# Softmax attention on one core: where the small products stand between the maxima

## The chip, the cores and the metric

The kernel runs on one core of a Trainium2 chip. The metric is the device time of one execution in microseconds (us); lower is better. Engines: PE is TensorE, DVE is VectorE, ACT is ScalarE, POOL is GpSimd, SP is SyncE.

## The reference

A decoder block of two layers over 1024 tokens (2 sequences of 512) of width 512, in float32. Six parts follow each other, each as `x = x + part(layernorm(x))`: a gated mixer, cross attention (softmax), a mixture of experts, decayed linear attention, linear cross attention, and a block-scaled feed forward. The change is in the second part:

```
q = qdq(x) @ qdq(wq).T + bq;  k, v = split(ctx @ wkv.T + bkv)      # 16 heads of 32, 1024 keys for each sequence
attn = softmax(q k^T / sqrt(32));  o = attn @ v
out = qdq(o) @ qdq(wp).T + bp        # qdq: each row to int8 by its largest magnitude, and back
x = x + out                          # then the layernorm of the experts
```

## The kernel before

**Groups, pairs, super-steps.** `cross_attention` (from L679) works on 8 groups `g`: sequence `g // 4`, four heads each. A group is two pairs of heads, so there are 16 pairs. A pair has 8 tiles of 128 keys for each of two heads. A *super-step* is 4 tiles of scores; a group has 8 super-steps, the whole attention 64 (numbered 0 to 63 here). A *slot* is half a super-step: super-step s has slots 2s and 2s+1, a group 16 slots.

**What PE does in a super-step** (the loop `for ss in range(NSS + 1)`, just after L1098): two score products (L1084), the jobs of slot 2s, two score products, the jobs of slot 2s+1, and then the eight products of probabilities and values (`weigh`, L1098) of the super-step before. ACT takes the exponential of each score tile (L1220) from a ring of three PSUM banks.

**The jobs.** The scores need the row maxima of the logits one group ahead. For that there are 16 units `max` for each group: PE makes 128x1024 logits (two products, L844), DVE reduces them to 128 maxima (L856, `b_nm`). In slots 10 to 105 nearly every slot has one. Other jobs use the same banks: `turn` (PE transposes the maxima of a group, L851; DVE splits them, L864 and L866, and ends with a small memset, L869), `pair` (four transposes of a finished pair's result, L1068; DVE divides by the sums, L1474 and L1477), `spread`, `oturn` (four transposes of the rounded output of a token tile, L1030; DVE copies them, L1465), `oproj` (the output projection of a token tile, four bf16 products, L1035; DVE scales it, L1406), `xturn` (four transposes of a normalised token tile, L1042; DVE copies them, L1469). `oturn`, `oproj` and `xturn` are those of tiles 0 to 3, the first sequence, which is finished halfway; the other four tiles come after the attention.

**The two job banks.** Jobs are numbered in the order of the list `JOBS`. Job j uses bank pair `2 * (j % 2)`, and PE may not start it before DVE has read job j-2:

```
if j >= 2:
    pe.wait_ge(job_read, j - 1)
```

PE and DVE both run through `JOBS` in order. After the jobs of a slot DVE does that slot's *step*, if `STEPS_AT` has one: the maxima of an output row, its scales, `rounded` (two operations, L1400 and L1403), `residual` (adds the projection to x, L1411), `stats` (L1415, L1417), `variance`, `normed` (L1425), `bias` (L1448), `most`. `oturn` waits on PE for `rounded` of its tile, `xturn` for `normed`. POOL takes the power for the normalisation in its turn for group 6, between two copies of values; SP sends the rows of maxima to the scores' operands after each `turn` (L836) and stacks the next group's operands (L826, L829).

**Placement before.** A slot's jobs are appended in the order `max`, `pair`, `turn`, `spread`, `oturn`, `oproj`, `xturn`. Slots counted from 64 (group 4): `oturn` of tiles 0 to 3 in 11, 12, 13, 14; `oproj` in 15, 17, 19, 21; `xturn` in 37, 38, 39, 40. The `turn` of the next group stands in the 13th slot of a group (12 counted from 0), behind that slot's `max`; the first of them in slot 13.

Of the kernel before, what the change touches and what calls it, by code (L numbers as in the profile page):

```python
# [678 lines left out]
def cross_attention(c):  # L679
# [70 lines left out]
    NG, QT = len(GROUPS), BANK // P  # L750
# [15 lines left out]

    SLOTS = 2 * TURNS_PER * 2
    LEAD, TURN_AT = 6, 12
    JOBS, JOBS_AT = [("max", 0, u) for u in range(UNITS)] + [("turn", 0, 0)], []
    FIRST_JOBS = len(JOBS)  # L770

    def first_slot(g, u):
        return SLOTS * (g - 1) - LEAD + u if g > 1 else 1 + 12 * u // UNITS

    for slot in range(2 * NSS + 5):
        g, here = slot // SLOTS, len(JOBS)
        JOBS += [("max", gg, u) for gg in range(1, NG) for u in range(UNITS) if first_slot(gg, u) == slot]
        q = (slot - 3) // (2 * TURNS_PER) - 1
        if slot == 2 * (TURNS_PER * (q + 1) + 1) + 1 and 0 <= q < PAIRS:
            JOBS.append(("pair", q, 0))  # L780
        if g + 1 < NG and slot % SLOTS == (TURN_AT if g else 13):
            JOBS.append(("turn", g + 1, 0))
        if slot == 20:
            JOBS.append(("spread", 0, 0))
        if g == 4 and 11 <= slot % SLOTS < 15:
            JOBS.append(("oturn", slot % SLOTS - 11, 0))
        if slot in range(4 * SLOTS + 15, 4 * SLOTS + 23, 2):
            JOBS.append(("oproj", (slot - 4 * SLOTS - 15) // 2, 0))
        if g == 6 and 5 <= slot % SLOTS < 9:
            JOBS.append(("xturn", slot % SLOTS - 5, 0))  # L790
        JOBS_AT.append(range(here, len(JOBS)))
    LAST_PAIR = len(JOBS) - 1


    STEPS_AT = {4 * SLOTS + at: step for at, step in
                [(4 + t, ("maxima", t)) for t in range(4)] + [(8, ("scales", 0))] + [(9 + t, ("rounded", t)) for t in range(4)]
                + [(16 + 2 * t, ("residual", t)) for t in range(4)] + [(23 + t, ("stats", t)) for t in range(4)]
                + [(27, ("variance", 0))] + [(34 + t, ("normed", t)) for t in range(4)]
                + [(60 + t, ("most", 4 + t)) for t in range(4)]
                + [(24 + 2 * t - 4 * SLOTS, ("bias", t)) for t in range(TT)]}  # L800

# [5 lines left out]
    added, stats_done, aggr_done, var_done, rstd_done, normed = (  # L807
        c.sem(f"c_ln_{n}") for n in ("added", "stats_done", "aggr_done", "var_done", "rstd_done", "normed"))
# [2494 lines left out]


STAGES = [mixer, cross_attention, linear_attention, mx_feed_forward]


# [77 lines left out]
```

## Time and profile before

| | us |
|---|---|
| median of 3 runs | 1894.0 |
| lowest and highest | 1892.58, 1895.92 |
| the profiled execution, its own time | 1895.18 |
| span from the first to the last instruction in it | 1893.4 |

| engine | busy us | share of the span |
|---|---|---|
| PE | 1833.2 | 97% |
| DVE | 1229.8 | 65% |
| ACT | 713.2 | 38% |
| POOL | 376.7 | 20% |

Times in rows are counted from the span's start. Busy time on PE is modelled: matmuls are pipelined, and a row's duration holds the tail of its last matmul, under which the next instruction can start already. So the distance between two starts says what an instruction really takes, and an idle time is shorter than the delay it stands for. "x8" is eight instructions merged into a row; a few per cent of matmul records can be missing, so that a row says x3 where four were run. Attention's super-steps lie between 304.8 and 595.4 us.

### The profile page before, as it was taken

What the parts mean: (1) busy time and instruction counts of PE and PEld (TensorE: products, weight loads), DVE (VectorE), ACT (ScalarE), POOL (GpSimd) and SP (SyncE); (2) the same over time, 40 slices, a digit from 0 to 9 for tenths busy, and PEclk for the clock granted to TensorE, in tenths of its full rate; (3) what the DMA queues carried; (4) which work ended last, traced back from release to release, by engine and by line L of the source; (5) the groups of instructions that cost most, each with busy time, mean ns of one, the idle gap of its engine ahead of it and who ended that gap; (6) DMA issues with size and microseconds to landing.
All of it is one profiled execution on the core that took longest, in us unless ns stands there. A gap on an engine that the chain in (4) does not pass through costs nothing. (4 is left out here: it accounts for less than half of the span.)

```text
span 1893.4 us, 24735 instructions
## 1 busy us (share of the span) xinstructions
PE 1833.2 (97%) x9384; PEld 1381.7 (73%) x9388; DVE 1229.8 (65%) x2114; ACT 713.2 (38%) x1151; POOL 376.7 (20%) x286
## 2 busy tenths in 40 slices
PE   8999999999899999999999999999999999999998
PEld 6888786444344688678887888887888865888886
DVE  6435665666743666686787786787782367666656
ACT  4302333455354588533333333332344332322211
POOL 0000011121100488511211211211110001144532
PEclk9999999999999899999999999999999999999999
DMA  6102323233314111232314313314112110110101
GB/s 223 45 1 72 100 63 80 53 76 76 96 26 134 34 68 57 89 120 53 100 40 121 102 40 124 100 40 137 49 65 78 69 45 22 45 45 23 45 1 45
DMA packets 109049, 132.67 MB, mean 70 GB/s; under 512 B 36066, under 2 KB 72930, under 8 KB 107394
## 3 DMA queue, kind: packets, MB, share of 16 engines
q1 hardware_dynamic: 108932, 131.10, 22.6%
q8 instruction: 75, 1.23, 0.3%
q14 instruction: 42, 0.34, 0.1%
HBM read 97.27 MB, written 14.75 MB: 59 GB/s over the span
## 5 line engine op out<-in xcount | busy, mean ns | idle before, releaser
L856 DVE TENSOR_REDUCE b_nm<-ps 128x1 f32<-128x1024 f32 x128 | 153.5, 1220 | 82.2 <-PE ps L844 82.2
L1220 ACT ACTIVATE b_pr<-ps 128x512 f32<-128x512 f32 x256 | 133.4, 602 | 127.7 <-PE ps L1084 127.4
L253 PE MATMUL ps<-d_x_high,d_w_high 128*128 128x512 f32 x384 | 154.3, 402 | 1.7 <-issue 1.7
L255 PE MATMUL ps<-d_x_high,d_w_low 128*128 128x512 f32 x384 | 149.8, 390 | 0.0
L254 PE MATMUL ps<-d_x_low,d_w_high 128*128 128x512 f32 x384 | 149.7, 390 | 0.0
L2487 POOL TENSOR_TENSOR d_sqsum<-d_sqsum,d_sq 128x512 f32<-128x512 f32 x32 | 45.1, 1409 | 474.4 <-ACT d_sq L2398 474.2
L1098 PE MATMUL ps<-b_pr,b_VS 128*64 128x512 f32 x512 | 123.8, 605 | 0.0
L1810 POOL TENSOR_TENSOR c_h<-c_h,c_w_row 128x512 f32<-128x512 f32 x64 | 105.5, 1658 | 29.6 <-DVE c_h L1825 20.3
L1084 PEld LDWEIGHTS ps<-b_qS,b_kS 98*128 98x128 f32 x256 | 42.6, 188 | 69.5 <-issue 49.5
L1084 PE MATMUL ps<-b_qS,b_kS 98*128 98x512 f32 x256 | 90.5, 435 | 2.8 <-ACT b_pr L1220 2.6
L844 PE MATMUL ps<-b_kS,b_qS 96*128 96x512 f32 x256 | 81.6, 402 | 7.8 <-DVE b_nm L856 6.2
L253 PEld LDWEIGHTS ps<-d_x_high,d_w_high 128*128 128x128 f32 x384 | 72.2, 188 | 17.4 <-issue 2.1
L255 PEld LDWEIGHTS ps<-d_x_high,d_w_low 128*128 128x128 f32 x384 | 72.1, 188 | 15.5
L254 PEld LDWEIGHTS ps<-d_x_low,d_w_high 128*128 128x128 f32 x384 | 72.3, 188 | 13.5
L1098 PEld LDWEIGHTS ps<-b_pr,b_VS 128*64 128x64 f32 x512 | 31.1, 136 | 55.5 <-issue 51.2
L1825 DVE TENSOR_TENSOR c_h<-ps,c_sq 128x512 f32<-128x512 f32 x64 | 44.3, 692 | 41.6 <-PE ps L255 24.7
L2380 ACT ACTIVATE d_kF<-ps 128x512 f32<-128x512 f32 x32 | 19.1, 598 | 131.9 <-PE ps L255 131.9
L844 PEld LDWEIGHTS ps<-b_kS,b_qS 96*128 96x128 f32 x256 | 46.4, 190 | 22.1 <-DVE b_nm L856 13.6
L3240 ACT ACTIVATE f_hF_high<-ps 128x512 fp32r<-128x512 f32 x32 | 19.1, 599 | 115.2 <-PE ps L3084 115.2
L2608 DVE TENSOR_TENSOR d_y<-ps,d_y 128x512 f32<-128x512 f32 x48 | 33.2, 692 | 43.9 <-PE ps L255 43.9
L3062 DVE TENSOR_TENSOR f_h<-ps,f_silu 128x512 f32<-128x512 f32 x32 | 21.8, 680 | 55.5 <-PE ps L255 32.2
L2281 PE MATMUL ps<-d_A,d_v 128*64 128x128 f32 x512 | 49.6, 284 | 4.4 <-DVE d_S L2562 4.4
(466 smaller groups left out, 4968.5 us busy)
## 6 DMA issues: line engine op xcount, KB each, us to landing
b_kS<-b_k_parts SPq DMA_DIRECT2D x96, 128.0 KB, 2.3
f_rows<-d_fw SPq DMA_DIRECT2D x24, 512.0 KB, 2.8
f_w<-f_rows SPq DMA_DIRECT2D x12, 1024.0 KB, 4.8
c_w_row<-w_rows SPq DMA_DIRECT2D x16, 512.0 KB, 3.6
b_qS<-b_q_parts SPq DMA_DIRECT2D x96, 64.0 KB, 2.0
d_w<-in_d_wq SPq DMA_DIRECT2D x16, 256.0 KB, 2.9
d_w<-in_d_wk SPq DMA_DIRECT2D x16, 256.0 KB, 3.0
d_w<-in_d_wg SPq DMA_DIRECT2D x16, 256.0 KB, 3.7
```

The source lines that it names most:

```text
L253: nc.tensor.matmul(out, lhsT[0], rhs[0], start=start, stop=False)
L254: nc.tensor.matmul(out, lhsT[0], rhs[1], start=False, stop=False)
L255: return nc.tensor.matmul(out, lhsT[1], rhs[0], start=False, stop=stop)
L844: last = nc.tensor.matmul(c.ps[:, banks + n, :], qS[s_][0:96, h, t * P:(t + 1) * P], kS[s_][0:96, h, n * BANK:(n + 1) * BANK], start=True, ...
L856: nc.vector.tensor_reduce(nm[:, g % 2, u:u + 1], c.ps[:, banks:banks + 2, :], AX.XY, ALU.max, negate=True).then_inc(job_read, 1)
L1084: nc.tensor.matmul(c.ps[:, 4 + n % BANKS, :], kS[g % 2][0:98, h, k * P:(k + 1) * P], qS[g % 2][0:98, h, :], start=True, stop=True).then_in ...
L1098: last = nc.tensor.matmul(c.ps[2 * DH * hh:2 * DH * (hh + 1), 7, :], VS[:, 2 * (q % 2) + hh, k * VW:k * VW + VPAD], pr[:, (n + hh) % RING, :],
L1220: nc.scalar.activation(pr[:, n % RING, :], c.ps[:, 4 + n % BANKS, :], ACT.Exp).then_inc(exp_done, 1)
L1810: nc.gpsimd.tensor_tensor(h[j % HR][:], h[j % HR][:], head.w_row[e % 2][:, n * BANK:(n + 1) * BANK], ALU.mult).then_inc(hw_done, 1)
L1825: nc.vector.tensor_tensor(h[j % HR][:], c.ps[:, 2 + j % 2, :], sq[:, j % 2, :], ALU.mult).then_inc(h_done, 1)
L2281: last = nc.tensor.matmul(c.ps[hh * D:(hh + 1) * D, 6 + b, col], v[:, t, h * D:(h + 1) * D], A[:, b, hh, ch, :], start=ch == 0, stop=True, ...
L2487: nc.gpsimd.tensor_tensor(sqsum[:, tok], sqsum[:, tok], sq[:, b, :], ALU.add).then_inc(sqsum_done, 1)
```

## The change

Three things. First, `turn`, `oturn`, `oproj` and `xturn` are appended ahead of the slot's `max`, not behind it. Second, they get even slots, so that at most one of them stands in a super-step, between its first two score products and its first `max`. Counted from slot 64: `oturn` 10, 14, 16, 18; `oproj` 20, 22, 24, 26; `xturn` 46, 48, 50, 52 (where no `max` is left). The turns of the maxima keep their slots. Third, DVE's steps behind them move: `residual` to 21, 23, 25, 29; `stats` to 31, 33, 37, 39; `variance` to 40; `normed` to 42 to 45. `pair` jobs stay where they were, behind the second `max`. The instructions of the kernel are the same in number and form.

```diff
     LEAD, TURN_AT = 6, 12
+    OTURN_AT, OPROJ_AT, XTURN_AT = (10, 14, 16, 18), (20, 22, 24, 26), (46, 48, 50, 52)
...
     for slot in range(2 * NSS + 5):
         g, here = slot // SLOTS, len(JOBS)
+        if g + 1 < NG and slot % SLOTS == (TURN_AT if g else 13):
+            JOBS.append(("turn", g + 1, 0))
+        if slot - 4 * SLOTS in OTURN_AT:
+            JOBS.append(("oturn", OTURN_AT.index(slot - 4 * SLOTS), 0))
+        if slot - 4 * SLOTS in OPROJ_AT:
+            JOBS.append(("oproj", OPROJ_AT.index(slot - 4 * SLOTS), 0))
+        if slot - 4 * SLOTS in XTURN_AT:
+            JOBS.append(("xturn", XTURN_AT.index(slot - 4 * SLOTS), 0))
         JOBS += [("max", gg, u) for gg in range(1, NG) for u in range(UNITS) if first_slot(gg, u) == slot]
         q = (slot - 3) // (2 * TURNS_PER) - 1
         if slot == 2 * (TURNS_PER * (q + 1) + 1) + 1 and 0 <= q < PAIRS:
             JOBS.append(("pair", q, 0))
-        if g + 1 < NG and slot % SLOTS == (TURN_AT if g else 13):
-            JOBS.append(("turn", g + 1, 0))
         if slot == 20:
             JOBS.append(("spread", 0, 0))
-        if g == 4 and 11 <= slot % SLOTS < 15:
-            JOBS.append(("oturn", slot % SLOTS - 11, 0))
-        if slot in range(4 * SLOTS + 15, 4 * SLOTS + 23, 2):
-            JOBS.append(("oproj", (slot - 4 * SLOTS - 15) // 2, 0))
-        if g == 6 and 5 <= slot % SLOTS < 9:
-            JOBS.append(("xturn", slot % SLOTS - 5, 0))
...
-                + [(16 + 2 * t, ("residual", t)) for t in range(4)] + [(23 + t, ("stats", t)) for t in range(4)]
-                + [(27, ("variance", 0))] + [(34 + t, ("normed", t)) for t in range(4)]
+                + [(at, ("residual", t)) for t, at in enumerate((21, 23, 25, 29))]
+                + [(at, ("stats", t)) for t, at in enumerate((31, 33, 37, 39))]
+                + [(40, ("variance", 0))] + [(42 + t, ("normed", t)) for t in range(4)]
```

## Rows read from the trace of the kernel before

**Rows 1.** Windows: stretch, its length, busy us of each engine, granted clock, DMA.

```profile
470.95:553.92 82.97, 74.41 (x323) 34.76 (x323) 58.63 (x83) 35.48 (x68) 9.76 (x13) 1.00 0.29 74
595.40:700.00 104.60, 104.02 (x420) 70.75 (x420) 69.23 (x126) 64.86 (x102) 52.56 (x30) 0.95 0.30 93
```

**Rows 2.** Waits of PE in 470.95 to 553.92: total, times, longest.

```profile
PE ps L1030 <- DVE b_nm L856: 2.5, 2, 1.3
```

**Rows 3.** Timeline of PE: an undisturbed super-step (34 to 35), start and duration.

```profile
463.05 0.73 PE L1084 MATMUL ps<-b_qS,b_kS 98*128 98x512 f32 x2
463.63 0.63 PE L844 MATMUL ps<-b_kS,b_qS 96*128 96x512 f32 x2
465.13 1.94 PE L1098 MATMUL ps<-b_pr,b_VS 128*64 128x512 f32 x8
467.00 0.73 PE L1084 MATMUL ps<-b_qS,b_kS 98*128 98x512 f32 x2
```

**Rows 4.** Timeline of PE: super-step 37, its oturn, and the start of 38.

```profile
475.46 0.40 PE L1030 MATMUL ps<-identb,b_oq 128*128 128x128 bf16 x4 [1.33 <-DVE b_nm L856]
...
477.65 0.73 PE L1084 MATMUL ps<-b_qS,b_kS 98*128 98x512 f32 x2
```

**Rows 5.** Timeline of DVE: the operations of jobs and steps.

```profile
471.29 0.50 DVE L1403 TENSOR_SCALAR b_oq<-b_o 128x512 bf16<-128x512 f32 x1
...
474.18 1.22 DVE L856 TENSOR_REDUCE b_nm<-ps 128x1 f32<-128x1024 f32 x1
...
493.63 0.74 DVE L1406 SCALAR_TENSOR_TENSOR b_tmp<-ps,b_so,b_swp_row 128x512 f32<-128x512 f32 x1
...
559.44 0.06 DVE L869 MEMSET b_mark<- 1x1 f32 x1
```

**Rows 6.** Timeline of PE: an oproj and the weigh behind it.

```profile
492.04 1.04 PE L1035 MATMUL ps<-b_wpT,b_oqF 128*128 128x512 bf16 x4 [0.38 <-DVE b_nm L856]
493.01 1.94 PE L1098 MATMUL ps<-b_pr,b_VS 128*64 128x512 f32 x8
```

**Rows 7.** Timeline of PE: starts of super-steps 45 and 46; 45 has a pair.

```profile
515.45 0.73 PE L1084 MATMUL ps<-b_qS,b_kS 98*128 98x512 f32 x2
...
520.42 0.73 PE L1084 MATMUL ps<-b_qS,b_kS 98*128 98x512 f32 x2
```

**Rows 8.** Timeline of PE: super-step 14 with its turn; later group 7's.

```profile
371.32 0.73 PE L1084 MATMUL ps<-b_qS,b_kS 98*128 98x512 f32 x2
...
373.83 0.73 PE L844 MATMUL ps<-b_kS,b_qS 96*128 96x512 f32 x2 [0.74 <-DVE b_nm L856]
...
376.36 0.74 PE L1084 MATMUL ps<-b_qS,b_kS 98*128 98x512 f32 x2
...
558.48 0.27 PE L851 MATMUL ps<-ident,b_nm 128*16 128x128 f32 x1
```

**Rows 9.** Timeline of PE: super-step 6 with the turn of group 1.

```profile
337.31 0.74 PE L844 MATMUL ps<-b_kS,b_qS 96*128 96x512 f32 x2 [0.39 <-DVE b_nm L856]
338.44 0.28 PE L851 MATMUL ps<-ident,b_nm 128*16 128x128 f32 x1 [0.40 <-DVE b_nm L856]
338.65 1.94 PE L1098 MATMUL ps<-b_pr,b_VS 128*64 128x512 f32 x8
```

**Rows 10.** Timeline of PE: an xturn and the scores behind it (super-step 51).

```profile
544.34 0.60 PE L1042 MATMUL ps<-ident,xn 128*128 128x128 f32 x4
544.70 0.71 PE L1084 MATMUL ps<-b_qS,b_kS 98*128 98x512 f32 x2
```

**Rows 11.** Timeline of PE: super-step 55, after the last max, and the next.

```profile
561.39 0.96 PE L1084 MATMUL ps<-b_qS,b_kS 98*128 98x512 f32 x3
562.58 0.49 PE L1084 MATMUL ps<-b_qS,b_kS 98*128 98x512 f32 x1 [0.22 <-ACT b_pr L1220]
...
564.87 0.96 PE L1084 MATMUL ps<-b_qS,b_kS 98*128 98x512 f32 x3
```

**Rows 12.** Windows after the attention, with the granted clock.

```profile
625.00:630.00 5.00, 5.00 (x21) 4.58 (x22) 2.53 (x3) 3.96 (x4) 2.07 (x1) 0.50 0.00 0
```

## The prediction

> **What bounds the kernel now.** I read the page first: PE is busy 97% of the span, so only what PE does or waits for can move the end. The windows come next: super-steps 37 to 52 are the stretch from 470.95 to 553.92, 82.97 us with 74.41 of PE busy, while DVE has 58.63 [rows 1]. In such a stretch the reader should look at the waits: two `oturn` alone wait 2.5 us there for DVE's maxima [rows 2]. Last, the timeline gives the yardstick. An undisturbed super-step takes 467.00 - 463.05 = 3.95 us, and its first maximum starts 463.63 - 463.05 = 0.58 after it [rows 3]. Sixteen of these would be 63.2 us, so the stretch holds 82.97 - 63.2 = 19.8 us of extras: four `pair`, two `turn`, four `oturn`, four `oproj`, four `xturn`, and the waits among them.
>
> **Why it waits.** A job needs DVE to have read the job before the last. DVE wants about 1.2 us for a maximum [rows 5]; two maxima fill 2.4 of the 3.95 us, so single ones never hold PE up. But a small job behind a maximum follows it on PE after half a microsecond and then needs the reading of the other bank, and DVE's step lies before that reading too. In super-step 37 three jobs and a step come together: `oturn` starts only at 475.46 after 1.33 us idle, and the super-step lasts 477.65 - 470.95 = 6.70 us, 2.75 over [rows 1, 4]. Put before the first maximum, a job has the `weigh` products (465.13 to 467.00, 1.87 us) and two scores (0.58) between it and the last job, 2.4 us in which DVE catches up [rows 3].
>
> **Own cost of each job on PE**, from starts:
> - `oproj`: 493.01 - 492.04 = 0.97 us [rows 6].
> - `xturn` between maximum and scores: 544.70 - 544.34 = 0.36 us [rows 10]; before `weigh` I take 0.5, between that and its row's 0.60.
> - `oturn`: bf16, row 0.40 us long [rows 4]. It lies between 0.2 (the 0.60 row of `xturn` costs 0.36, so 0.24 of a row is tail) and 0.4; I take 0.25.
> - `turn`: one matmul, 0.27 us long [rows 8], nearly all tail: 0.03.
> - `pair`: super-step 45 lasts 520.42 - 515.45 = 4.97, so 1.02 each with its wait; it stays in place and keeps it [rows 7].
>
> **The stretch before, split.** 4 pairs 4.1, 4 oproj 3.9, 4 oturn 1.0, 4 xturn (two at 0.36, two at 0.5) 1.7, turns 0.1: 10.8 us. Of 19.8 that leaves 9.0 us of waits.
>
> **The stretch after, by super-steps.**
> - 37 (`oturn` 0; two maxima; pair): the products are ready at 470.95 + 0.58 = 471.53, but `oturn` needs `rounded` of tile 0, which ends 471.29 + 0.50 = 471.79 [rows 5], so 0.3 of wait. DVE then has a copy (about 0.4), a maximum, `rounded` (about 0.95), a maximum, the pair's two operations. The pair waits only for the first maximum, at about 473.95, and `weigh` follows 0.6 later; 5.5 us in all.
> - 38 (`turn` 5, no `oturn`): DVE is still behind with `rounded`, and reaches the turn's reading about 0.1 late: 4.3 us.
> - 39 (`oturn` 1): DVE reads the last maximum of 38 to 0.9 after the start of 39; the first maximum waits 0.15: 4.4 us.
> - 40 and 41 (`oturn` 2, 3): 3.95 + 0.25 = 4.2, and with the pair 5.2.
> - 42 to 44 (`oproj` 0 to 2): 3.95 + 0.97 = 4.9 each. DVE's scaling (0.74 [rows 5]) starts when the product ends and is over as the second maximum comes up, so no wait. DVE has two maxima 2.4, scaling 0.7, `residual` 0.6 in it, 3.7 of 4.9.
> - 45 (`oproj` 3, pair): 4.97 + 0.97, and 0.2 because the scaling delays the maximum for which the pair waits: 6.1.
> - 46 (`turn` 6): 4.1. 49 has its pair, 4.97. The six others (47, 48, 50, 51, 52 and no `xturn` any more) are five at 3.95: 19.75.
>
> Sum: 5.5 + 4.3 + 4.4 + 4.2 + 5.2 + 14.7 + 6.1 + 4.1 + 4.97 + 19.75 = 73.2 us. Gain 82.97 - 73.2 = **9.8 us**: 8.0 of waits, the rest the `xturn`s gone elsewhere.
>
> **The xturns' new place** (super-steps 55 to 58). There a super-step lasts 564.87 - 561.39 = 3.48 us and PE waits 0.22 for ACT before the fourth score [rows 11]. An `xturn` of 0.36 between the score pairs uses that wait up: 0.14 is left. Bounds 0 and 0.5; four times 0.1 to 0.14 is **+0.4 us** (up to 2.0). Its `normed` comes four slots earlier on a DVE without maxima, so it never waits. POOL's power is released later by `variance` (slot 104, not 91), and behind it in POOL's queue stand only the values of pair 14, whose buffer is not free before super-step 53; cost nothing. No DMA moves but the rows of maxima behind `turn`, which go out earlier. SP's loads of the next operands hang on scores that come sooner too; the nearest deadline is group 7's first stacking, released in super-step 43 and needed in 45, and there `oproj` gives it 9.8 us where it had 7.9. Bound: 0 to 1.2 us, I take 0.
>
> **The turns of groups 2, 3, 4** (turns 5 and 6 are counted). Super-step 14 lasts 376.36 - 371.32 = 5.04 us, 1.09 over, because the second maximum stands at 373.83 and waits for the turn's reading, which DVE can do only after the first maximum [rows 8]. In front, DVE reads the turn at once (group 7's turn, with no maximum about, starts at 558.48 and its reading is over at 559.44 + 0.06, 1.02 us later [rows 5, 8]), and the second maximum comes 0.03 + 0.47 + 0.57 = 1.07 after it. So 4.0 us, gain 1.05 each: **-3.1 us** for three. If DVE is 0.3 later it is 2.2.
>
> **The turn of group 1** stands in an odd slot. Now the maximum starts at 337.31 and the turn at 338.44 [rows 9]. Swapped, the maximum gets the later start, and 0.5 to 0.65 lie between it and `weigh` instead of 338.65 - 338.44 = 0.21: **+0.4 us**.
>
> **Sum**: -9.8 + 0.4 - 3.1 + 0.4 = -12.1 us, taken as -12. Behind the attention PE is busy 104.02 of 104.60 us [rows 1], so the rest shifts as a whole. The profiled execution, 1895.2 us of its own time (1.8 over its span), would come to 1883.2; it stood 1.2 over the median of 1894.0, so the forecast for the median is **1882 us**. Own range 1879 to 1885: turns 0.9 less, `oturn` and DVE's lag 1.5 either way, xturns up to 1.6 more, loads up to 1.2.
>
> **Where the clock could come in.** All of 470.95 to 553.92 has clock 1.00 [rows 1]; after the attention the row at 625 to 630 shows 0.50, the 1.2 GHz level, behind transposes between products of 16 columns [rows 12]. Such a fall of some 8 us comes again and may take 4 us more or less with where it falls.
>
> The Trainium skill ("TensorE: Matmul & The Clock Gate", Part 4: PE-mode transpose) says that transposes do not count as busy for the clock in the way that products do; by that rule the change spreads transposes into the stretch paced by ACT, where PE has the least work. No row of that stretch shows it; it is the last rival below.
>
> **Rivals.**
> 1. *DVE becomes the bound between slots 74 and 93.* For: rounding, copies and two maxima make 0.4 + 2.4 + 0.95 (twice at worst) on DVE in a super-step of 4.2, so each maximum may carry a lag over. Against: 58.63 of 82.97 us busy [rows 1]. Eight super-steps losing 0.7 more each: 5.6 less gained, 1887.6 us.
> 2. *The gain is given back* by something with a time of its own behind the attention, as weights that arrive late. Against: PE's 104.02 of 104.60. Time: 1894. That the order doesn't change what PE waits for would show the same.
> 3. *The clock falls in super-steps 55 to 63*, the other side. At 0.50 the `weigh` (1.87) and the four scores (0.96) double: 2.8 us for each super-step. It decides from the fifth such super-step on (12 / 2.8 = 4.3); with all ten from 554 on the price is 28: 1910 us. For: `pair`s there already put transposes beside a wait of 0.22, and now four more come. Against: four times 0.36 us is little in 40 us.
>
> **How the numbers follow.** Forecast 0.68, rival 1 0.19, rival 2 0.06, rival 3 0.05, something slower otherwise 0.02. What a measurement can tell is 0.2%, 3.8 us. Faster: the forecast, rival 1 but a sliver: 0.86; same 0.07; slower 0.07. The range takes in half of rival 1 above and the clock's luck below: 1877.5 to 1888.5.
>
> **What would show it.** PE's waits on `b_nm` at L1030, L1035 and at L844 behind `turn` go from 9 us to near 1; super-step 14 goes to 4.0; those with `oproj` to 4.9; 37 to 5.5; xturns cost under 0.2. It is wrong if the super-steps with a job in front last over 0.5 longer than I say (rival 1), if the attention is 12 us shorter and the end is not (rival 2), or if the clock shows 0.50 before 595 (rival 3).

## The result, and the profile after

The median went from 1894.1 to **1880.5 us**; the ratio is 0.9926 with a 95% interval of 0.9907 to 0.9945, that is 10 to 18 us faster. One of the four executions after the change took 9052.4 us at a granted clock of 0.189, for a reason that no profile shows, and is left out of the ratio; the other three took 1877.3, 1880.3 and 1880.8. The forecast was 1882. The profiled execution took 1877.3 us (span 1875.5).

Lines after the change stand two lower than before (L844 is L846, L856 L858, L1030 L1032, L1035 L1037, L1042 L1044, L1068 L1070, L1084 L1086, L1098 L1100). First the windows of super-steps 37 to 52, to be set against [rows 1]. Columns: stretch, length, busy us of PE, of the weight loads (PEld), of DVE, ACT and POOL, granted clock, DMA share, GB/s:

```profile
468.24:541.67 73.43, 71.58 (x307) 33.12 (x307) 54.39 (x76) 35.97 (x68) 9.39 (x13) 1.00 0.33 83
```

The stretch lasts 73.43 us where it lasted 82.97, with four xturns fewer in it. PE is busy for all but 1.85 us of it; before, 8.56 us were idle. PE's waits in that stretch, all there are, against [rows 2]:

```profile
PE ps L1070 <- DVE b_nm L858: 1.5, 4, 0.4
PE ps L1032 <- DVE b_oq L1405: 0.3, 1, 0.3
```

No `oturn` and no `oproj` waits for maxima any more. What is left are the pairs (L1070), which the change did not touch, and one `oturn` for its rounding. The timeline of PE shows super-step 37, then 38, against [rows 4]:

```profile
468.24 0.73 PE L1086 MATMUL ps<-b_qS,b_kS 98*128 98x512 f32 x2
469.23 0.38 PE L1032 MATMUL ps<-identb,b_oq 128*128 128x128 bf16 x4 [0.26 <-DVE b_oq L1405]
469.42 0.71 PE L846 MATMUL ps<-b_kS,b_qS 96*128 96x512 f32 x2
469.97 0.63 PE L1086 MATMUL ps<-b_qS,b_kS 98*128 98x512 f32 x2
470.44 0.63 PE L846 MATMUL ps<-b_kS,b_qS 96*128 96x512 f32 x2
471.45 0.66 PE L1070 MATMUL ps<-ident,b_oT 128*128 128x128 f32 x4 [0.38 <-DVE b_nm L858]
472.04 1.94 PE L1100 MATMUL ps<-b_pr,b_VS 128*64 128x512 f32 x8
473.90 0.73 PE L1086 MATMUL ps<-b_qS,b_kS 98*128 98x512 f32 x2
```

The idle of 1.33 before `oturn` is now 0.26, and the super-step went from 6.70 to 5.66 us. In super-step 14, with rows of PE, PEld and DVE, the turn stands first and DVE reads it ahead of the maximum (against [rows 8]):

```profile
371.57 0.73 PE L1086 MATMUL ps<-b_qS,b_kS 98*128 98x512 f32 x2
...
372.14 0.27 PE L853 MATMUL ps<-ident,b_nm 128*16 128x128 f32 x1
...
372.17 0.71 PE L846 MATMUL ps<-b_kS,b_qS 96*128 96x512 f32 x2
...
372.76 0.28 DVE L868 TENSOR_TENSOR b_nm_parts<-ps,b_nm_parts 16x128 fp32r<-16x128 f32 x1
...
373.08 1.22 DVE L858 TENSOR_REDUCE b_nm<-ps 128x1 f32<-128x1024 f32 x1
373.09 0.06 DVE L871 MEMSET b_mark<- 1x1 f32 x1
373.20 0.30 PEld L846 LDWEIGHTS ps<-b_kS,b_qS 96*128 96x128 f32 x2 [0.27 <-DVE b_mark L871]
373.21 0.73 PE L846 MATMUL ps<-b_kS,b_qS 96*128 96x512 f32 x2
...
373.87 1.94 PE L1100 MATMUL ps<-b_pr,b_VS 128*64 128x512 f32 x8
...
375.74 0.73 PE L1086 MATMUL ps<-b_qS,b_kS 98*128 98x512 f32 x2
```

The reading ends at 373.15, and the second maximum starts 0.06 later. PE shows no idle there, but the load of its weights waits 0.27 us for the reading: the maximum still comes a little late, and the super-step lasts 4.17 us, not 4.0. And an xturn in super-step 55 (against [rows 11]):

```profile
549.14 0.73 PE L1086 MATMUL ps<-b_qS,b_kS 98*128 98x512 f32 x2
549.71 0.60 PE L1044 MATMUL ps<-ident,xn 128*128 128x128 f32 x4
550.07 0.76 PE L1086 MATMUL ps<-b_qS,b_kS 98*128 98x512 f32 x2
550.75 1.94 PE L1100 MATMUL ps<-b_pr,b_VS 128*64 128x512 f32 x8
552.62 0.73 PE L1086 MATMUL ps<-b_qS,b_kS 98*128 98x512 f32 x2
```

552.62 - 549.14 = 3.48 us, as long as without the xturn; the wait for ACT is gone.

**The yardstick for the experiments.** Outside low-clock stretches the length of a super-step repeats from trace to trace to 0.03 us in all but a few places, so the traces say far more than the times. I take the *attention length*: from the first score product to the first product of the experts' logits. Before, the rows are

```profile
304.78 0.86 PE L1084 MATMUL ps<-b_qS,b_kS 98*128 98x512 f32 x3
...
595.47 1.06 PE L1618 MATMUL ps<-c_wgT,xF 128*128 128x16 f32 x8
```

which is 290.69 us; after, 304.63 to 583.20, 278.57 us. (Gains of 12.3 us and marks at 595.5 and 583.2 in the expectations below are the ends alone, without the starts.)

### The profile page after: what moved, and what is told of

Same layout as the page of the kernel before. It is cut to its first block and busy times, and to the rows that moved or that the text cites. A ratio compares the mean times of both kernels' runs of the same rounds, so it can differ in the third digit from the quotient of the medians.

```text
span 1875.5 us, 24735 instructions
## 1 busy us (share of the span) xinstructions
PE 1826.5 (97%) x9384; PEld 1377.2 (73%) x9388; DVE 1229.1 (66%) x2114; ACT 713.6 (38%) x1151; POOL 376.8 (20%) x286
## 5 line engine op out<-in xcount | busy, mean ns | idle before, releaser
L858 DVE TENSOR_REDUCE b_nm<-ps 128x1 f32<-128x1024 f32 x128 | 152.3, 1219 | 59.3 <-PE ps L846 58.7
L1100 PE MATMUL ps<-b_pr,b_VS 128*64 128x512 f32 x512 | 123.8, 605 | 0.0
L1086 PEld LDWEIGHTS ps<-b_qS,b_kS 98*128 98x128 f32 x256 | 43.1, 188 | 66.7 <-issue 47.9
L1086 PE MATMUL ps<-b_qS,b_kS 98*128 98x512 f32 x256 | 89.9, 432 | 1.8 <-ACT b_pr L1222 1.7
L846 PE MATMUL ps<-b_kS,b_qS 96*128 96x512 f32 x256 | 83.3, 409 | 3.5 <-DVE b_nm L858 2.3
L1100 PEld LDWEIGHTS ps<-b_pr,b_VS 128*64 128x64 f32 x512 | 31.2, 136 | 56.0 <-issue 45.6
L846 PEld LDWEIGHTS ps<-b_kS,b_qS 96*128 96x128 f32 x256 | 45.6, 190 | 17.4 <-DVE b_nm L858 6.7
L2539 DVE TENSOR_TENSOR d_A<-ps,d_mask 128x512 f32<-128x512 f32 x64 | 41.0, 682 | 19.0 <-issue 11.3
```

The lines of the kernel that those rows point to most:

```text
L846: last = nc.tensor.matmul(c.ps[:, banks + n, :], qS[s_][0:96, h, t * P:(t + 1) * P], kS[s_][0:96, h, n * BANK:(n + 1) * BANK], start=True, ...
L858: nc.vector.tensor_reduce(nm[:, g % 2, u:u + 1], c.ps[:, banks:banks + 2, :], AX.XY, ALU.max, negate=True).then_inc(job_read, 1)
L1086: nc.tensor.matmul(c.ps[:, 4 + n % BANKS, :], kS[g % 2][0:98, h, k * P:(k + 1) * P], qS[g % 2][0:98, h, :], start=True, stop=True).then_in ...
L1100: last = nc.tensor.matmul(c.ps[2 * DH * hh:2 * DH * (hh + 1), 7, :], VS[:, 2 * (q % 2) + hh, k * VW:k * VW + VPAD], pr[:, (n + hh) % RING, :],
L2539: nc.vector.tensor_tensor(A[:, b, hh, :, :], c.ps[:, 2 + j % 2, :].rearrange("p (c i) -> p c i", i=P), mask[:, p % 3, hh, :].unsqueeze(1). ...
```

## The experiments

Seven experiments follow. The ratio is to the kernel before, measured beside each; "attention" is the length just defined, in the one profiled execution; "cleared gain" is the gain in it without the excess that a low-clock stretch or a single odd super-step shows against the other traces with the same work there. The kernel before has 0.36 of such excess in super-step 33 (5.32 us; 4.96 to 4.98 in the six others with the same work, 5.24 in turns alone) and 0.2 in super-step 41 (7.30 us; 7.10 and 7.09 in the two others with the same work), so it is 290.1 cleared. The cleared gains are good to 0.1 or 0.2 us.

| kernel | median us | ratio, 95% interval | attention | cleared gain | expected gain |
|---|---|---|---|---|---|
| the change | 1880.5 | 0.9926, 0.9907 to 0.9945 | 278.57 | 11.6 | 12.1 |
| the change again | 1881.5 | 0.9915, 0.9894 to 0.9935 | 280.35 | 11.4 | 12.3 |
| turns alone | 1890.5 | 0.9985, 0.9973 to 0.9996 | 288.45 | 3.5 | 4.3 |
| oturn and oproj alone | 1887.4 | 0.9972, 0.9960 to 0.9984 | 286.24 | 3.9 | 4.0 |
| xturns alone | 1889.1 | 0.9983, 0.9970 to 0.9996 | 286.38 | 3.8 | 3.7 |
| order alone | 1887.9 | 0.9969, 0.9959 to 0.9980 | 290.65 | 5.7 | 9 |
| slots alone | 1884.6 | 0.9934, 0.9909 to 0.9959 | 284.02 | 6.1 | 4.7 |
| pairs in front too | 1876.6 | 0.9887, 0.9867 to 0.9908 | 273.30 | 16.8 | 19.5 |

The first four experiments below were measured together (before: 1893.3), the last three together at another time (before: 1897.2), the result by itself (before: 1894.1); times of different groups can't be compared.

**Turns alone.** The turn's lines ahead of the `max` line, all else as before:

```diff
+        if g + 1 < NG and slot % SLOTS == (TURN_AT if g else 13):
+            JOBS.append(("turn", g + 1, 0))
         JOBS += [("max", gg, u) for gg in range(1, NG) for u in range(UNITS) if first_slot(gg, u) == slot]
...
-        if g + 1 < NG and slot % SLOTS == (TURN_AT if g else 13):
-            JOBS.append(("turn", g + 1, 0))
```

> Of the change only the first part: the turn of the maxima stands ahead of its slot's max, in all seven groups; oturn, oproj, xturn and the steps stay as before. The mark is the first product of the experts' logits on PE, at 595.5 us before and 583.2 after the whole change. Theory A (a small job costs its wait because DVE has not yet read the other bank, and the place ahead of the first max takes the wait away, each job by itself): turns 2, 3 and 4 give 1.05 us each, turn 6 0.9, turn 5 about 0.7 (an oturn still stands behind it), turn 1 loses 0.4: the mark comes 4.3 us earlier, at 591.2, super-step 14 lasts 4.0 instead of 5.04, and the time is about 1889.8. Rival B (the gain comes only from taking the jobs into super-steps of their own; the turns changed none): the mark stays at 595.5, time 1894.

The four super-steps with a turn and nothing else lasted 4.16 or 4.17 instead of 5.05 us, 0.88 each; super-step 38 gained 0.37, super-step 6 lost 0.45: 3.4 us. Rival B is out, as no job moved to another super-step. In this trace super-step 37, whose work is unchanged, took 8.26 us and not 6.70. The windows (columns: stretch, length, PE busy, granted clock, DMA) and the timeline show why:

```profile
465.00:470.00 5.00, 5.00 (x22) 1.00 0.62 144
470.00:475.00 5.00, 3.37 (x16) 0.75 0.05 13
475.00:480.00 5.00, 4.43 (x23) 0.91 0.02 3
```

```profile
472.60 0.61 PE L1030 MATMUL ps<-identb,b_oq 128*128 128x128 bf16 x4 [1.33 <-DVE b_nm L856]
473.14 3.29 PE L1098 MATMUL ps<-b_pr,b_VS 128*64 128x512 f32 x8
```

Behind the old idle of 1.33 us the clock was below its upper level for a while (0.75 and 0.91 on average), and `weigh` took 3.29 us instead of 1.94.

**Oturn and oproj alone.** `OTURN_AT` and `OPROJ_AT` as in the change, ahead of `max`; turns and xturns as before:

```diff
-                + [(16 + 2 * t, ("residual", t)) for t in range(4)] + [(23 + t, ("stats", t)) for t in range(4)]
-                + [(27, ("variance", 0))] + [(34 + t, ("normed", t)) for t in range(4)]
+                + [(at, ("residual", t)) for t, at in enumerate((21, 23, 25, 27))] + [(28 + t, ("stats", t)) for t in range(4)]
+                + [(32, ("variance", 0))] + [(34 + t, ("normed", t)) for t in range(4)]
```

> Of the change only oturn and oproj of the first four token tiles, in the new slots and ahead of the max; residual in 21, 23, 25, 27, stats in 28 to 31 and variance in 32, so that the xturns can stay in 37 to 40; turns as before. Theory A: super-steps 37 to 45 together 49.5 before and 44.6 after the whole change, of which 0.9 is turn 5's: 4.0 us, mark at 591.5, time about 1890. Rival B expects more here than of the turns, all that the turns do not give: 8 us. Rival C (DVE is the bound here with rounding, copies and maxima): under 2 us.

3.9 us cleared, 0.9972 in time (5.3, with 3.0 to 7.6 in the interval): theory A, and rival C (under 2 us) is out, and B (8 us) too. Super-steps 39 to 45 have the lengths of the change to 0.01 us; 38, which keeps its turn behind the maximum, took 5.04.

**Xturns alone.** Only `XTURN_AT` from the change:

```diff
+        if slot - 4 * SLOTS in XTURN_AT:
+            JOBS.append(("xturn", XTURN_AT.index(slot - 4 * SLOTS), 0))
         JOBS += [("max", gg, u) for gg in range(1, NG) for u in range(UNITS) if first_slot(gg, u) == slot]
...
-        if g == 6 and 5 <= slot % SLOTS < 9:
-            JOBS.append(("xturn", slot % SLOTS - 5, 0))
```

> Of the change only the xturns, moved from slots 37 to 40 to 46, 48, 50, 52, where no max is left; everything else as before. Theory A: super-steps 50 to 52 lose their extras (1.03 + 1.61 + 1.10 = 3.7 us) and 55 to 58 take the xturns for nothing, since they fill PE's wait for ACT: mark at 591.8, time about 1890.3. If an xturn costs its own 0.36 there, the gain is 2.3 us. Rival D (transposes in the thin stretch bring the clock down to 0.50 before 595 us): the mark later than before. The three parts together should be the 12.3 us of the whole change, 4.3 + 4.0 + 3.7 = 12.0, if they are independent.

Super-steps 50 to 52 gave 3.7 us, which is the whole of it within 0.1, and 55 to 58 took nothing (3.48, 3.48, 3.99, 3.49, as before to 0.01). The clock between 553 and 580 us:

```profile
553.00:580.00 27.00, 26.15 (x115) 1.00 0.01 1
```

It stayed at the upper level, 1.00, and did so in all nine traces; rival D is out as far as these show it. By the rule of the Trainium skill ("TensorE: Matmul & The Clock Gate", Part 4: PE-mode transpose) the added transposes should not have counted as work in the way that products do; this case neither contradicts it nor shows it, for the stretch is still full of products.

The three parts make 3.5 + 3.9 + 3.8 = 11.2 us, the whole 11.6. They are independent but for super-step 38, which before holds a turn and two `oturn` jobs: the turn in front gave 0.37 there, the `oturn` jobs gone 0.89, both together 1.76, 0.5 more than the sum.

**Order alone.** All four kinds ahead of `max`, in their old slots and with the old steps:

```diff
+        if g + 1 < NG and slot % SLOTS == (TURN_AT if g else 13):
+            JOBS.append(("turn", g + 1, 0))
+        if g == 4 and 11 <= slot % SLOTS < 15:
+            JOBS.append(("oturn", slot % SLOTS - 11, 0))
+        if slot in range(4 * SLOTS + 15, 4 * SLOTS + 23, 2):
+            JOBS.append(("oproj", (slot - 4 * SLOTS - 15) // 2, 0))
+        if g == 6 and 5 <= slot % SLOTS < 9:
+            JOBS.append(("xturn", slot % SLOTS - 5, 0))
         JOBS += [("max", gg, u) for gg in range(1, NG) for u in range(UNITS) if first_slot(gg, u) == slot]
```

> Order alone: turn, oturn, oproj and xturn ahead of the slot's max, but in their old slots (also odd ones, and two in one super-step), and with the old steps. Theory A: ahead of a second max a job itself no longer waits, but the max behind it does, for the reading of the first max (1.9 us from its start, against 0.47 + 0.57 + the job's own time), so oturn and xturn keep about 0.5 us of wait each there and oproj, itself 0.97 long, none: gain about 9 us, mark at 586.5, time about 1885. Rival B (own super-steps are what counts): under 4 us. Rival E (order is all): the full 12.3 us, mark at 583.2.

The trace says 290.65, no gain, but super-steps 5 and 6 took 12.27 and 8.46 us where they take 8.37 and 6.18 otherwise (granted clock 0.74 from 320 to 340). The excess starts with a transfer that came late, not with the clock:

```profile
329.28 1.17 PE L844 MATMUL ps<-b_kS,b_qS 96*128 96x512 f32 x2 [1.76 <-DMA b_qS<-b_q_parts]
```

This product starts 3.42 us into super-step 5; in the other traces it starts after 2.53 to 2.82. The first job that the edit moves stands behind it, in super-step 6, so it is put down to the single execution; the low clock follows. Without that 6.2 it is 5.7 cleared, and the time says 1893.3 x 0.0031 = 5.9 (3.8 to 7.8). So E is out, B (under 4 us) is out by the trace and at the edge of the interval by the time, and A is right in kind but 3 us too generous. The timeline of super-step 38 shows where waits are left:

```profile
480.15 0.73 PE L1084 MATMUL ps<-b_qS,b_kS 98*128 98x512 f32 x2
480.72 0.27 PE L851 MATMUL ps<-ident,b_nm 128*16 128x128 f32 x1
480.83 0.38 PE L1030 MATMUL ps<-identb,b_oq 128*128 128x128 bf16 x4
481.79 0.74 PE L844 MATMUL ps<-b_kS,b_qS 96*128 96x512 f32 x2 [0.57 <-DVE b_mark L869]
482.37 0.63 PE L1084 MATMUL ps<-b_qS,b_kS 98*128 98x512 f32 x2
482.85 0.40 PE L1030 MATMUL ps<-identb,b_oq 128*128 128x128 bf16 x4
483.85 0.73 PE L844 MATMUL ps<-b_kS,b_qS 96*128 96x512 f32 x2 [0.60 <-DVE b_nm L856]
```

No small job waits, but both maxima do: the first for the reading of the turn two jobs ahead of it, the second for the reading of the first. So the super-step takes 6.23 us, longer than the 5.93 before.

**Slots alone.** The change with its four kinds of jobs behind `max` and `pair`:

```diff
         JOBS += [("max", gg, u) for gg in range(1, NG) for u in range(UNITS) if first_slot(gg, u) == slot]
         q = (slot - 3) // (2 * TURNS_PER) - 1
         if slot == 2 * (TURNS_PER * (q + 1) + 1) + 1 and 0 <= q < PAIRS:
             JOBS.append(("pair", q, 0))
+        if g + 1 < NG and slot % SLOTS == (TURN_AT if g else 13):
+            JOBS.append(("turn", g + 1, 0))
+        if slot - 4 * SLOTS in OTURN_AT:
+            JOBS.append(("oturn", OTURN_AT.index(slot - 4 * SLOTS), 0))
...
```

> Slots alone: oturn, oproj, xturn and the steps in the slots of the change, but all jobs behind their slot's max, the turns too. The mark (first product of the experts' logits) is at 595.5 us before and 583.2 after the change. Theory A: behind the first max an oturn does not wait but the second max does, as in super-step 14 before, about 0.7 us each for four oturns; the turns gain nothing (4.5 us less than the change); oproj, 0.97 long, covers its wait; xturns as in the change. Mark at about 590.8, gain 4.7 us, time about 1889.5. Rival B (own super-steps are what counts): the full 12.3 us. Rival E (order is all): about 0.

6.1 us cleared, neither the full gain nor none. Of these 3.7 are the `xturn` jobs in super-steps 50 to 52, which in this kernel too stand where no maximum is left, and 2.4 are `oturn` and `oproj` in 37 to 45. Super-step 39:

```profile
482.86 0.73 PE L1086 MATMUL ps<-b_qS,b_kS 98*128 98x512 f32 x2
483.43 0.63 PE L846 MATMUL ps<-b_kS,b_qS 96*128 96x512 f32 x2
483.89 0.40 PE L1032 MATMUL ps<-identb,b_oq 128*128 128x128 bf16 x4
484.10 0.71 PE L1086 MATMUL ps<-b_qS,b_kS 98*128 98x512 f32 x2
485.37 0.73 PE L846 MATMUL ps<-b_kS,b_qS 96*128 96x512 f32 x2 [0.56 <-DVE b_nm L858]
```

The second maximum waits, 5.04 us against 4.23 in the change; with `oproj` the two placements differ by 0.05 only (5.03 to 5.06 against 4.99), since the projection's own 0.97 us covers the reading. In time the kernel did better than its trace: 12.6 us between the medians, with 8 to 17 in the interval, against 6.1. So did the two others of its group (pairs in front too 20.6 against 16.8, the change again 15.7 against 11.4): the kernel before took 1897.2 us beside them, 3.9 more than beside the first four, and why isn't known. Against the change measured beside it this kernel is 3.1 us behind, where the traces say 5.5; its six executions scatter over 10 us. For the share of the slots I go by the trace.

**Pairs in front too.** The change carried to the one job it left behind the second maximum, spread so that still only one job stands in front in a super-step:

```diff
+    OTURN_AT, OPROJ_AT, XTURN_AT = (10, 16, 18, 20), (24, 26, 32, 34), (46, 48, 50, 52)
+    PAIR_AT = (14, 22, 30, 36, 46, 52, 62, 68, 78, 86, 94, 100, 107, 115, 123, 131)
...
+        if slot in PAIR_AT:
+            JOBS.append(("pair", PAIR_AT.index(slot), 0))
         JOBS += [("max", gg, u) for gg in range(1, NG) for u in range(UNITS) if first_slot(gg, u) == slot]
...
+                + [(at, ("residual", t)) for t, at in enumerate((25, 27, 33, 36))]
+                + [(at, ("stats", t)) for t, at in enumerate((29, 31, 35, 39))]
```

> The change carried further: pairs 0 to 11 too stand ahead of a super-step's first max, alone there, in slots 14, 22, 30, 36, 46, 52, 62, 68, 78, 86, 94, 100; oturn goes to 10, 16, 18, 20, oproj to 24, 26, 32, 34 (counted from 64), residual to 25, 27, 33, 36, stats to 29, 31, 35, 39. Theory A: a pair costs 1.02 us behind the second max (5.3 in 41 against 4.2) and about 0.4 ahead of the first, so twelve times 0.6: the mark at 576 instead of 583.2, time about 1873. Rival F (the pair's own transposes are the cost, its wait is not): at most 2 us. Rival G (ACT's moving of the next pair's result waits for the later pair and holds the exponentials up): slower than the change.

1876.6 us, 4.8 below the change measured beside it, ratio 0.9887 (0.9867 to 0.9908): it is faster than both kernels. The attention is 5.3 us shorter than in the change. Rivals F and G are out. A super-step with a pair in front:

```profile
407.03 0.73 PE L1086 MATMUL ps<-b_qS,b_kS 98*128 98x512 f32 x2
407.60 0.60 PE L1070 MATMUL ps<-ident,b_oT 128*128 128x128 f32 x4
407.95 0.71 PE L846 MATMUL ps<-b_kS,b_qS 96*128 96x512 f32 x2
408.50 0.63 PE L1086 MATMUL ps<-b_qS,b_kS 98*128 98x512 f32 x2
408.97 0.72 PE L846 MATMUL ps<-b_kS,b_qS 96*128 96x512 f32 x2
409.62 1.94 PE L1100 MATMUL ps<-b_pr,b_VS 128*64 128x512 f32 x8
411.49 0.73 PE L1086 MATMUL ps<-b_qS,b_kS 98*128 98x512 f32 x2
```

4.46 us, 0.5 over the bare super-step, and where the pair left the super-step keeps 0.06 to 0.1 for ACT's copy of the result (4.01 to 4.05). So a pair went from 1.02 to about 0.6, not to the 0.4 I had put down.

**The change again.**

> The changed kernel once more, for the part of the gain behind the attention. In the profiled execution of the change the mark was 12.3 us earlier and the end 17.9, and the difference came in three places where the clock's low stretches were shorter. Theory A: this is a matter of the single execution; the time lies 12.3 us under before on average (1881.8) with a scatter of some 2 us, and the mark in this profile is at 583.2 again. Rival H (the shift itself takes low stretches away for good): 1877 again, with a mean clock of 0.997.

The time is 1881.5 and the mean clock of the profiled execution 0.995, as theory A has them. But H is not out: beside the kernel before, which took 1897.2 here and not 1894, the gain is 15.7 us (12 to 20), which holds H's 17 and has A's 12.3 at its edge; and the mean clock of the six executions is 0.995 against 0.993 of the eleven before. In the first group, where the kernel before was measured 33 times, the gains by time (order alone 5.9, `oturn` and `oproj` alone 5.3, xturns alone 3.2, turns alone 2.8) make 17.2 together where the traces have 5.7, 3.9, 3.8 and 3.5, 16.9 together: nothing is left over there. My mark of 583.2 did not come back (586.9): the attention began 1.9 us later, and super-step 6 took 7.66 us instead of 6.18. The windows show a low clock behind the waits of the turn (0.47 us idle) and of the maximum (0.77 us idle) in it:

```profile
335.00:340.00 5.00, 3.89 (x17) 1.00 0.00 0
340.00:345.00 5.00, 4.87 (x13) 0.66 0.02 3
```

From the logits to the end of the span the nine traces have 1290.9 to 1297.9 us, for the same instructions. Before has the longest of these, 1297.9, the change 1292.3 and 1292.7, the pairs kernel 1297.3. So the 5.6 us that the first profile of the change gained behind the attention lie within the scatter of single executions.

## Why the prediction was right

| step | forecast us | measured |
|---|---|---|
| super-step 37 | 5.5 | 5.66 |
| 38, 39 | 4.3, 4.4 | 4.17, 4.23 |
| 40, 41 | 4.2, 5.2 | 4.22, 5.27 |
| 42 to 44 (oproj), each | 4.9 | 4.99 |
| 45, 46 | 6.1, 4.1 | 6.04, 4.17 |
| 47, 48, 50 to 52 together; 49 | 19.75; 4.97 | 19.73; 4.98 |
| stretch 37 to 52 | 73.2 | 73.43 |
| xturns in 55 to 58 | +0.4 | 0.0 |
| turns 2, 3, 4 | -3.1 | -2.6 |
| turn 1 | +0.4 | +0.44 |
| attention length | -12.1 | -12.1 (cleared -11.6) |

- *What the wait is* (the reading of the job before the last) held: each part alone gave its own share but for the 0.5 us in super-step 38, and PE's waits for maxima at L1030 and L1035 vanished.
- *DVE's lag in 38 and 39* was put 0.15 too high, and *37* 0.16 too low: the pair waits for a maximum delayed by the rounding. The three `oproj` super-steps were put 0.26 too low together; with these the forecast of the stretch is 0.2 too short.
- *The turns* were put at 4.0 us and are 4.17; the second maximum starts at 373.21, 1.07 us after the turn, just where the forecast had it. But without the wait it would follow after 0.98 (an undisturbed one starts 464.58 - 463.63 = 0.95 after the first, and the turn takes 0.03), and the 4.0 left out this 0.09. `weigh` then comes another 0.66 later instead of 0.55. The load of this product's weights starts at 373.20, 0.01 ahead of it, where in the undisturbed super-step it starts 0.2 ahead; that this costs the 0.11 was not tested. The bound with DVE 0.3 later (2.2) held it.
- *The xturns* cost nothing, the lower bound.
- *Loads and POOL* cost nothing, as taken.
- *Behind the attention* everything shifted as a whole, but with a scatter of 7 us between executions, about the 4 either way that were allowed for the clock. The 11.6 us of the cleared traces lie within the interval of 10 to 18 around the 13.6 between the medians; whether a part of the rest is real stays open, the more so as the change again gained 15.7 (12 to 20) beside a kernel before that took 1897.2. One candidate is the idle of 1.33 us in super-step 37, which the change removes: behind it one of the three traces that keep it (turns alone; not before, not xturns alone) shows the clock low, at a price of 1.6 us. But the change also puts an idle of 0.77 us into super-step 6, where before none was over 0.40, and behind that one trace (the change again) shows the clock low as well, at the same price. How often either happens was not measured.
- *Luck*: that the attention came out 12.1 us shorter, as forecast to 0.1, is partly chance. The terms measured 9.5 + 2.6 - 0.4 + 0.0 = 11.7 us, against 9.8 + 3.1 - 0.4 - 0.4, and 0.36 more came from the odd super-step 33 of the one trace before (another 0.2, in the 9.5, from its super-step 41); the turns' smaller gain was made up by the xturns' smaller cost.
- *Slips that change nothing*: "the six others" of the stretch are five; and the row of 0.96 us in rival 3 holds three scores, so at half clock a super-step would lose about 3.0 us, not 2.8.
- Of the rivals, 1 (DVE) and 3 (the clock in 55 to 63) are refuted by the lengths of the super-steps and by the clock of 1.00 there; 2 by the times. H, that the change takes low-clock stretches away for good, is neither shown nor refuted.

## What to carry to other kernels

Where two engines hand two buffers back and forth, a job costs its own time only if the consumer's work for the job before last fits under what the producer does in between; so put small jobs behind the producer's longest stretch that needs no buffer, one for each round, and ask for the item behind the job too, not for the job alone. Order alone gave 5.7 us here and the new slots alone 6.1 (3.7 of it by moving jobs to where no maximum is left), together 11.6. Work it out by the starts of a repeating round, not by idle times: in super-steps 37 to 52 PE's idle fell by 8.56 - 1.85 = 6.7 us, and the stretch became 9.5 us shorter, of which only 1.7 is the estimated work of the `xturn` jobs that left it.

## What was not expected of the hardware

- The same super-step repeats to 0.03 us from execution to execution, and yet the whole kernel scatters over 12 us (before: 1887.2 to 1899.0 in 33 runs). In the traces the scatter that could be traced within the attention sits in stretches of low clock that start behind short idles of PE and fall in other places each time: three of the nine traces have one, behind idles of 1.33, 0.77 and 1.76 us, costing 1.6, 1.6 and 6.2 us (the last with 0.6 to 0.9 of a late transfer). The same idles of 1.33 and 0.77 us stand in other traces at a clock of 1.00.
- Four transposes put into a place where PE waits 0.22 us for ACT cost nothing although they hold PE for 0.36. By starts, the fourth score stood 562.58 - 561.39 = 1.19 us behind the first, and at their pace (0.57 for two) it would stand 0.86 behind: an estimated delay of 0.33, more than the idle shown, and the transposes fill it. `weigh` starts 1.61 us into the super-step with them and without.
